# The output product moved to the seam between two stages, and the last expert's lower product carried into the next heads' stage

## What is computed

```python
    h = layernorm(x, ln_g, ln_b)
    q, k, v = heads(h @ Wq), heads(h @ Wk), heads(h @ Wv)
    q = l2norm(q) * q_scale
    k = l2norm(k) * k_scale
    logits = jnp.einsum('bhid,bhjd->bhij', q, k) * QK_SCALE
    attn = jax.nn.softmax(jnp.where(causal, logits, NEG_INF), axis=-1)
    out = jnp.einsum('bhij,bhjd->bhid', attn, v)
    out = out.transpose(0, 2, 1, 3).reshape(B, S, H * DH) @ Wo
    h = layernorm(out, ln_g, ln_b)
    gate = jax.nn.softmax(h @ gate_w + gate_b, axis=-1)
    hid = jax.nn.gelu(jnp.einsum('bsd,edf->bsef', h, w1) + b1)
    exp_out = jnp.einsum('bsef,efd->bsed', hid, w2) + b2
    moe = jnp.einsum('bse,bsed->bsd', gate, exp_out)
    return layernorm(moe, ln_g, ln_b)
```

## Time and profile before

| | before |
|---|---|
| median of 3 runs | 1336.35 us (1336.09 to 1337.26) |
| the profiled execution, its own time | 1336.95 us |
| its span, first to last instruction | 1335.2 us |
| TensorE, products | 1166.4 us busy, 87% |
| TensorE, weight loads | 948.6 us, 71% |
| VectorE | 1017.0 us, 76% |
| ScalarE | 807.9 us, 61% |
| GpSimd | 243.2 us, 18% |
| TensorE's granted clock, mean | 0.931 |

### The profile page before, as it was taken

How to read it: one execution, slowest core, us unless ns; L and a number is a source line. 1 busy time by engine, 2 the same in 40 slices (tenths; PEclk the granted TensorE clock), 3 DMA queues, 4 the chain that set the end, 5 groups by cost and what they waited for, 6 DMA issues and landing times.

```text
span 1335.2 us, 27712 instructions
## 1 busy us (share of the span) xinstructions
PE 1166.4 (87%) x10435; PEld 948.6 (71%) x10435; DVE 1017.0 (76%) x2710; ACT 807.9 (61%) x1868; POOL 243.2 (18%) x283
## 2 busy tenths in 40 slices
PE   3685989897998989899897998989799898989978
PEld 1363768685876868687685877868587786858877
DVE  6669587787878778787877878788887878777652
ACT  5283756658475665747556574755747575575644
POOL 1131211303021030211203021130302113030100
PEclk9595999899999989989899998989999898999889
DMA  6001000000000000000000000000000000000000
GB/s 177 5 1 40 2 1 13 1 9 5 9 5 1 14 1 9 5 9 6 1 13 1 10 5 9 6 1 14 1 9 6 9 5 5 2 9 1 5 5 5
DMA packets 18723, 14.61 MB, mean 11 GB/s; under 512 B 2408, under 2 KB 16160, under 8 KB 18592
## 3 DMA queue, kind: packets, MB, share of 16 engines
q1 hardware_dynamic: 17680, 12.76, 3.3%
q10 hardware_dynamic: 912, 0.09, 0.1%
HBM read 10.75 MB, written 2.10 MB: 10 GB/s over the span
## 4 chain that ended last, share of the span: by engine, by line
PE 69%; ACT 13%; DVE 12%; issue 5%; POOL 0%; SPq 0%; DMA 0%; DVEq 0%; POOLq 0%; ACTq 0%
PE O L499 17%; PE O L415 8%; PE S L398 6%; PE U L431 4%; PE U L483 4%; PE U L484 4%; PE U L485 4%; PE J L344 4%; PE S L362 3%; DVE st L1108 3%; PE S L358 3%; PE J L309 2%; ACT P L676 2%; PE J L311 2%; PE J L310 2%
## 5 line engine op out<-in xcount | busy, mean ns | idle before, releaser
L703 ACT ACTIVATE hid<-U,b1c 128x256 f32<-128x256 f32 x512 | 202.3, 473 | 203.1 <-PE U L485 202.4
L499 PE MATMUL O<-w2s,hid 128*128 128x128 f32 x2048 | 251.5, 276 | 0.0
L499 PEld LDWEIGHTS O<-w2s,hid 128*128 128x128 f32 x2048 | 238.5, 192 | 2.9
L827 POOL TENSOR_SCALAR_AFFINE_SELECT P<-P 128x512 f32<-128x512 f32 x128 | 81.5, 637 | 871.2 <-ACT P L676 871.2
L415 PE MATMUL O<-Vx,P 128*128 128x66 f32 x1536 | 198.1, 279 | 16.5 <-ACT OT L682 16.3
L415 PEld LDWEIGHTS O<-Vx,P 128*128 128x128 f32 x1536 | 181.7, 192 | 32.8 <-issue 24.3
L1108 DVE TENSOR_TENSOR_SCAN st<-aexp,u 128x256 f32<-128x256 f32 x256 | 199.3, 778 | 4.8 <-ACT aexp L688 4.8
L819 POOL TENSOR_TENSOR raw<-raw,nr 128x512 f32<-128x512 f32 x128 | 141.4, 1133 | 141.1 <-DVE nr L981 114.7
L483 PE MATMUL U<-h2h,w1h 128*128 128x256 f16 x512 | 148.7, 290 | 0.2 <-ACT hid L703 0.2
L484 PE MATMUL U<-h2l,w1h 128*128 128x256 f16 x512 | 148.2, 289 | 0.0
L485 PE MATMUL U<-h2h,w1l 128*128 128x256 f16 x512 | 147.5, 288 | 0.0
(11 more groups left out here) (162 smaller groups left out, 2151.2 us busy)
## 6 DMA issues: line engine op xcount, KB each, us to landing
xin<-in_L_attn_x SPq DMA_DIRECT2D x16, 128.0 KB, 2.1
xres<-in_L_attn_x SPq DMA_DIRECT2D x16, 128.0 KB, 2.3
hid<-in_L_ffn_w SPq DMA_DIRECT2D x2, 1024.0 KB, 6.0
out_dram<-fin SPq DMA_DIRECT2D x16, 128.0 KB, 1.8
raw<-in_L_ffn_Wq SPq DMA_DIRECT2D x1, 512.0 KB, 4.4
raw<-in_L_ffn_Wk SPq DMA_DIRECT2D x1, 512.0 KB, 5.6
raw<-in_L_ffn_Wv SPq DMA_DIRECT2D x1, 512.0 KB, 6.6
wos<-in_L_ffn_Wo SPq DMA_DIRECT2D x1, 512.0 KB, 11.0
```

The source lines that it names most:

```text
L499: last = mm(O[e % 2][:, t * P:(t + 1) * P], hid[:, e % 2, m, t * P:(t + 1) * P], w2s[:, e * FC + m, :], start=(m == 0), stop=(m == FC - 1))
L703: fn(hid[:, e % 2, f % FC, :], U[q % 2][:, m * SEQ:(m + 1) * SEQ], ACT.Gelu_apprx_tanh, bias=b1c[:, f:f + 1], scale=1.0 / WS).then_inc(gel ...
```

## The change

The output product of sequence i moves out of the next body's steps 0 and 1 to the seam of its own body: TensorE has it at m = 0, behind the first two `turn_qk`, as one piece, and it writes S2 instead of U0. `output` therefore waits for the last exponentials (they read S2), and the first `scores_for_max` waits for the copy z2. `copy_output` moves to m = 0 on ScalarE, and `o_step` 0 and 1 to m = 9 on VectorE.

The lower product of the last expert, and its weighted sum, move from the end of the experts' stage to step k = 0 of the next body, and `turn_y` goes there as well, now through U1.

With these go the parts of the output norm and the gate: `turn_z2` from k = 6 to 3, `gate_logits` from 7 to 5, `root_o` from 4 to 0, `gate_exps` from 9 to 7, and VectorE's tables O_AT, E_AT and SCAN_AT. `o_step` 12 and 13 move from m = 0 to k = 8. The upper product of expert 0 is written at the end of k = 9 rather than at the start of m = 0, which is the same place. At the seam ScalarE has `copy_ot(7)` before the last two V copies and `high(0)` and `high(1)` before the table load and the gelus; VectorE has `low(0)` and `low(1)` before the norm steps.

The diff, cut to its core:

```diff
@@ tensor @@
                 if p == 0:
                     from_one(pe, ex_done, s * NP)
+                    from_one(pe, wo_copied, s)
...
-            def output(s, t, before):
-                if t == 0:
-                    pe.wait_ge(ot_done, (s + 1) * NP)
-                    if before:
-                        pe.wait_ge(gelu_done, s * NE * FC)
-                for m in range(HD // P):
-                    last = mm(U[0][:, t * P:(t + 1) * P], OT[:, m, t * P:(t + 1) * P],
...
+            def output(s):
+
+                pe.wait_ge(ot_done, (s + 1) * NP)
+                pe.wait_ge(ex_done, (s + 1) * NP)
+                for t in range(T):
+                    for m in range(HD // P):
+                        last = mm(S2[:, 0, t * P:(t + 1) * P], OT[:, m, t * P:(t + 1) * P],
...
             def turn_y(s):
                 pe.wait_ge(y_done, (s + 1) * DS)
-                pe.wait_ge(wo_copied, s + 1)
-                for t in range(T):
-                    last = tr(U[0][:, t * P:(t + 1) * P], y[:, s % 2, t * P:(t + 1) * P], ident[:, :])
+                from_one(pe, gelu_done, s * NE * FC)
+                for t in range(T):
+                    last = tr(U[1][:, t * P:(t + 1) * P], y[:, s % 2, t * P:(t + 1) * P], ident[:, :])
...
-                    if old and k < T:
-                        output(i - 1, k, older)
+                    if older and k == 0:
+                        expert_down(i - 2, NE - 1, i * NP)
+                    if old and k == 0:
+                        turn_y(i - 1)
                     if old and k == 3:
-                        turn_y(i - 1)
-                    if old and k == 6:
                         turn_z2(i - 1)
-                    if old and k == 7:
+                    if old and k == 5:
                         gate_logits(i - 1)
                     if k >= 2:
                         turn_o(i, k - 2)
+                    if old and k == 9:
+                        expert_up(i - 1, 0)
                 for m in range(NE + 2):
-                    if old and m == 0:
-                        expert_up(i - 1, 0)
                     if new and m in TURN_AT:
                         turn_qk(i + 1, TURN_AT[m])
                         turn_qk(i + 1, TURN_AT[m] + 1)
+                    if m == 0:
+                        output(i)
...
-                    if old and 1 <= m <= NE:
+                    if old and 1 <= m < NE:
                         expert_down(i - 1, m - 1, (i + 1) * NP)
@@ scalar @@
             def copy_output(s):
                 act.wait_ge(wo_ready, s + 1)
-                fn(z2[:, :, :].rearrange("p t d -> p (t d)"), U[0][:, 0:SEQ], ACT.Copy).then_inc(wo_copied, 1)
+                from_one(act, o_tr, s)
+                fn(z2[:, :, :].rearrange("p t d -> p (t d)"), S2[:, 0, 0:SEQ], ACT.Copy).then_inc(wo_copied, 1)
...
-                    if old and k == 2:
-                        copy_output(i - 1)
...
-                    if older and k == 0:
+                    if older and k == 1:
                         last_norm(i - 2)
-                    if old and k == 4:
+                    if old and k == 0:
                         root_o(i - 1)
...
-                    if old and k == 9:
+                    if old and k == 7:
                         gate_exps(i - 1)
+                copy_ot(i, NP - 1)
                 if new:
                     copy_v(i + 1, 2)
-                copy_ot(i, NP - 1)
-                if new:
                     copy_v(i + 1, 3)
                     norm_qk(i + 1, 1)
+                    high(i + 1, 0)
+                    high(i + 1, 1)
                 with_gelu_and_tanh()
...
+                    if m == 0:
+                        copy_output(i)
@@ vector @@
-            E_AT = {0: (0, 1), 1: (2, 3, 4), 2: (5, 6), 3: (7,)}
+            E_AT = {1: (0, 1), 2: (2, 3, 4), 3: (5, 6), 4: (7,)}
             G_AT = {0: (0, 1), 4: (2,), 8: (3, 4, 5)}
-            O_AT = {3: (0, 1), 5: (2, 3, 4, 5), 7: (6, 7, 8), 8: (9, 10, 11)}
-            SCAN_AT = {1: 0, 2: 1, 4: 2, 6: 3, 7: 4, 8: 5, 9: 6}
+            O_AT = {1: (2,), 2: (3, 4, 5), 4: (6, 7), 5: (8,), 6: (9, 10, 11), 8: (12, 13)}
+            SCAN_AT = {1: 0, 3: 1, 5: 2, 6: 3, 7: 4, 8: 5, 9: 6}
...
+                    if older and k == 0:
+                        add_expert(i - 2, NE - 1)
...
-                    if old and k == 5:
+                    if old and k == 4:
                         add_y(i - 1)
...
-                    if old and m == 0:
-                        o_step(i - 1, 12)
-                        o_step(i - 1, 13)
...
                         if new and m == 0:
+                            low(i + 1, 0)
+                            low(i + 1, 1)
                             norm_step(i + 1, 1, 1)
...
+                    if m == 9:
+                        o_step(i, 0)
+                        o_step(i, 1)
```

More of the change, by code:

```diff
@@ L423, in turn_o @@
                 last.then_inc(ot_ready, 1)
-            def output(s, t, before):
-                if t == 0:
-                    pe.wait_ge(ot_done, (s + 1) * NP)
-                    if before:
-                        pe.wait_ge(gelu_done, s * NE * FC)
-                for m in range(HD // P):
-                    last = mm(U[0][:, t * P:(t + 1) * P], OT[:, m, t * P:(t + 1) * P],
-                              wos[:, m, :], start=(m == 0), stop=(m == HD // P - 1))
-                if t == T - 1:
-                    last.then_inc(wo_ready, 1)
+            def output(s):
[4 more added lines that the diff above has]
+                        last = mm(S2[:, 0, t * P:(t + 1) * P], OT[:, m, t * P:(t + 1) * P],
+                                  wos[:, m, :], start=(m == 0), stop=(m == HD // P - 1))
+                last.then_inc(wo_ready, 1)
             def turn_y(s):
                 pe.wait_ge(y_done, (s + 1) * DS)
-                pe.wait_ge(wo_copied, s + 1)
+                from_one(pe, gelu_done, s * NE * FC)
                 for t in range(T):
-                    last = tr(U[0][:, t * P:(t + 1) * P], y[:, s % 2, t * P:(t + 1) * P], ident[:, :])
+                    last = tr(U[1][:, t * P:(t + 1) * P], y[:, s % 2, t * P:(t + 1) * P], ident[:, :])
                 last.then_inc(y_tr, 1)
@@ L444, in turn_z2 @@
                 pe.wait_ge(o_vec, s * KO + 10)
-                pe.wait_ge(xy_done, s + 1)
+                from_one(pe, gelu_done, s * NE * FC)
                 for t in range(T):
@@ L451, in gate_logits @@
                 pe.wait_ge(o_vec, s * KO + 11)
+                pe.wait_ge(xy_done, s + 1)
                 for t in range(T):
@@ L583, in tail @@
             def tail():
-                output(LAST, 0, True)
-                output(LAST, 1, True)
+                expert_down(LAST - 1, NE - 1, NSEQ * NP)
                 turn_y(LAST)
@@ L785, in body @@
                         gelus(i - 1, m)
-                    if new and m in TURN_AT:
+                    if m == 0:
+                        copy_output(i)
+                    if new and m > 0 and m in TURN_AT:
                         high(i + 1, TURN_AT[m])
@@ L798, in tail @@
                 last_norm(LAST - 1)
-                copy_output(LAST)
                 root_o(LAST)
@@ L1147, in add_y @@
                 from_one(dve, e_vec, s * KE)
-                V.tensor_tensor(xy[:, :, :].rearrange("p t d -> p (t d)"), U[0][:, 0:SEQ],
+                V.tensor_tensor(xy[:, :, :].rearrange("p t d -> p (t d)"), U[1][:, 0:SEQ],
                                 xb[:, :, :].rearrange("p t d -> p (t d)"), ALU.add).then_inc(xy_done, 1)
@@ L1248, in body @@
                 for m in range(NE + 2):
-                    if old and m == 0:
-                        o_step(i - 1, 12)
-                        o_step(i - 1, 13)
                     if old and m == 2:
                         o_step(i - 1, 15)
-                    if old and m >= 2:
+                    if old and 2 <= m <= NE:
                         add_expert(i - 1, m - 2)
@@ L1287, in body @@
                         step_inputs(i + 1, 1)
+                    if m == 9:
+                        o_step(i, 0)
+                        o_step(i, 1)
             def tail():
+                add_expert(LAST - 1, NE - 1)
                 for n in range(8):
@@ L1292, in tail @@
                 add_y(LAST)
-                for n in range(16):
+                for n in range(2, 16):
                     o_step(LAST, n)
```

## The result

The changed kernel takes **1253.08 us**, the median of four runs (1251.98 to 1255.17), beside 1336.22 for the kernel before: a ratio of 0.938, 95% interval 0.9363 to 0.9397. The prediction was 1266.7, in a range of 1250 to 1300. The profiled execution took 1251.98, with a span of 1250.3, so the span fell by 84.9, where the sum had 69.6.

The account below looks back on a forecast made before the run. TensorE sets the pace almost everywhere, except where it waits in the heads' last steps and at the seam. Gains 63.7 + 6.7 - 0.8 = 69.6 off 1336.95 give 1267.3, as median 1266.7; range 1250 to 1300.

Parts of the forecast that it names:

- VectorE's row up to gateT: Seam, before gated_b2: add_state, scan, add_state beside GpSimd's products take 3.7; with low(2), low(3), gateT is ready at 43.8.
- Steps 0 to 6 and 6 to 9: Heads' stage: scores of step 6 at 19.8 instead of 21.31, then VectorE's shorter row gives turn_o(7) at 33.0 instead of 35.96.
- The seam: Output product fills the 3.86 wait, ending wait and low clock; third turn_qk at 39.35 instead of 42.44.
- What is late next: Before gated_b2: a new wait of about 1.4 for gateT; gated_b2 at 43.9 instead of 47.87, 4.0 gained.
- Experts: From gated_b2 TensorE is dense, 27.93 unchanged; wait of about 1.5 for the maxima, next t = 0 at 73.65.
- Sum: Whole kernel: thirteen steady sequences gain 63.7, sequence 1 gains 6.7, sequence 0 nothing, the last loses 0.8; total 69.6.
- (a): TensorE's clock falls at the new waits, t = 0 and gated_b2, costing 39; 1306 us, chance 0.12.
- (b): ScalarE sets the heads' steps, 0.2 late in seven steps, 1.4 per sequence; 1285 us, chance 0.12.
- (c): Before gated_b2, GpSimd blocks VectorE more than taken, 1.2 per sequence, 17 us; 1284 us, chance 0.08.
- (d): New waits are smaller: VectorE instructions partly clear of GpSimd, maxima earlier; up to 1.2 less per sequence, 1251 us, chance 0.12.
- (e): Move doesn't fill the seam: low(0) not ready when the product ends, about 2 lost; 1300 to 1320 us, chance 0.04.
- (f): Slower than before: lower clock from t = 0 and from gated_b2 in every sequence; 1351 us, chance 0.04.

Follow-up runs that it names:

- experiment 5: Kernel before with only the new seam order: high(0), high(1) ahead of ScalarE's table load, low(0), low(1) ahead of VectorE's norm steps; 1332.7 us (0.9974).
- experiment 2: Changed kernel with the last expert's lower product put back to the end of the experts' stage on TensorE only; 1247.22 us (0.9347).
- experiment 7: Two separate edits of the changed kernel: copy gateT ahead of low(2), low(3), 1242.66 us; three norm steps moved behind scan 8 and its add, 1246.46 us.
- experiment 6: Kernel before with the new ScalarE and VectorE seam order, plus the copy gateT ahead of low(2) and low(3); 1291.92 us (0.967).
- second kernel of experiment 1: Changed kernel with seven eighths of the output product left out, so it computes less; 1251.19 us (0.9375).

## Why the prediction held, step by step

The mechanism held at every place. One term of the sum was mis-sized, VectorE's row up to gateT, and with it two announced figures were missed on the good side: a wait of 1 to 2 before gated_b2 (0.65) and a period of 73.3 to 74.1 (72.71).

| t in one steady sequence | before | predicted | after |
|---|---|---|---|
| scores of step 6 | 21.31 | 19.8 | 19.76 |
| turn_o(7) | 35.96 | 33.0 | 33.01 |
| first turn_qk | 37.54 | 34.6 | 34.59 |
| output product | | 35.6 | 35.47 |
| third turn_qk | 42.44 | 39.35 | 39.04 |
| gated_b2 | 47.87 | 43.9 | 42.86 |
| next t = 0 | 78.58 | 73.65 | 72.71 |

- **Steps 0 to 6 and 6 to 9**: right to a tenth. VectorE waits for the norm's root until 591.78 (t = 22.92; 19.8 + 3.16 was the step), and then works through to On(7) and turn_o(7) at 33.01. Against the kernel before, steps 0 to 6 gave 1.55 and steps 6 to 9, where h2T, h2h and h2l had left VectorE's row, another 1.40.
- **The seam**: right. The third turn_qk came 0.31 before the forecast, because the output product, 3.74 by its record, takes 3.57 from its start to the next one's. The wait for QTl and the low clock are gone, the product lies in their place, and the copy z, begun at 608.17 (t = 39.31), comes ahead of TensorE.
- **What is late next**: this is the step that failed in size. It announced a new wait of 1.4 for gateT, and the wait is 0.65, with gated_b2 1.04 earlier than worked out. The term was three instructions beside GpSimd's products, 3.7. Only two were: the first add_state started at 606.90, ahead of GpSimd's 607.07, and took 0.48; scan and second add took 1.53 and 1.08, as in the earlier trace rows. From start to end that is 3.05 instead of 3.7, and it began 0.26 earlier (t = 38.04 instead of 38.3). 0.9 of the 1.0 is that.
- **Experts**: right. The wait of 1.54 at t = 0 was forecast as 1.5.
- **Sum**, from the starts of the sequences in the two traces: thirteen steady sequences gave 74.8, 5.76 each, where 63.7 stood. The eleven microseconds are, in the main, the mis-sized term, 13 x 0.9. (The forecast took the 78.58 of one sequence for all; the thirteen took 78.48 on the mean, with the low clock in different places, which is 1.3 less to gain.) One sequence of the thirteen, at 277, took 73.72, with a wait of 1.66 before gated_b2. Sequence 1 gained 7.6 (6.7 forecast). Prologue and sequence 0 gained 1.0 (0, bounds -1 and +2). The last sequence with the tail gained 1.5, where a loss of 0.8 stood. In part that is the clock: before, it was low ahead of that sequence's gated_b2 (0.57 from 1256 to 1264), and after it is 1.00 there (1172 to 1181), and gated_b2 comes 1.0 earlier. The rest stays open. The wait before z2's transposes in the tail grew from 3.04 to 6.18, where it was forecast to shrink by 1: the output product no longer stands ahead of it.

**The rivals.** (a), the clock at the new waits, didn't come: 1.00 throughout with waits of 1.54 and 0.65. That it could was no idle thought: experiment 5 has waits of 1.50 and 2.38 at one seam, and the low clock behind them. (b), ScalarE in the heads' steps, cost nothing: TensorE's waits for OT in one sequence are 0.39 and 0.57 after, both where VectorE's row sets the pace, and were 0.34, 0.17 and 0.56 before; in the first steps one is seen only in experiment 2, at 0.34. (c), a whole GpSimd product in front of each VectorE instruction, fell: 0.85 and 0.60 were added, beside products of 1.01 (4.04 for four in experiment 7, where no scan or add lies beside them). (d), smaller waits, is what happened; its number was 1251, its chance 0.12, and one of its two reasons, instructions partly clear of GpSimd, was the right one; the other, the maxima done earlier, was not (1.54). (e) and (f) didn't come.

**The port that VectorE and GpSimd share.** The Trainium skill, "SBUF — State Buffer", section "SBUF: two separate sides", names the cases in which VectorE and GpSimd exclude each other, one of which is a VectorE instruction with two inputs in SBUF. The rows agree in kind: scan and add, with both inputs in SBUF, were stretched; QTl<-J,wcol,QTh, whose large input J is in PSUM, took 0.47 at 609.87 while GpSimd was still in its products, as it does without them (650.62 in the earlier trace rows, behind their end). That the loser fully blocks for the instruction would have put up to 1.01 in front of each; the rows have 0.85 and 0.60, and GpSimd itself lost 0.75 over the four products (4.79 against 4.04).

## What to carry to other kernels

A wait of the busiest engine that comes every round is room for work of that engine: a product that was priced at 3.1 per round in one place cost nothing in the other, and the cut of the same product in both kernels showed it. When such a wait is filled, price the row of the next engine instruction by instruction, and check the start of each against the start of its rival for the port, since one instruction that slipped ahead was 0.6 of the 1.0 by which gated_b2 was mis-timed. And don't judge an edit by the whole time while the clock of TensorE moves: the new order at the seam was worth 2.7 us of the kernel before alone and 43 us with one more line moved, and only half of the difference, 1.4 of 2.9 us per sequence, was the wait that this line shortened.

## What the runs showed of the hardware

- **The low clock can hide a gain.** In experiment 5 a gain of 2.05 per sequence, seen at gated_b2, ended as 0.5, because the stretch of low clock moved from a place where it cost 1.0 to dense products where it cost 1.5.
- **When it falls stays open.** TensorE had waited 0.54, 1.50 and 2.38 at the seam before it fell in experiment 5; with 0.54, 1.49 and 1.00, in experiment 6, it stayed at 1.00 in ten sequences in a row. Before the change it fell after waits of 0.55 and 3.86. But the waits of experiment 5 were followed by full clock in the sequence from 995.25, and there it had fallen a little after 1026, with no wait above 0.57 since that sequence began. In the second kernel of experiment 1 it fell behind waits of 1.05 and 1.28 in some sequences and not in others. So the length of one wait doesn't decide it.
- **A table load costs ScalarE 1.28 us here, and the next instruction starts at once** (605.43, then the gelu at 606.73; before, 643.41 and 644.71). The Trainium skill, "ScalarE: Activation LUTs", section "What ACT_TABLE_LOAD costs", puts a drain of about 1380 ns beside the load; neither trace shows one behind it.
- **VectorE beside GpSimd**: a scan of 256 columns 1.53 instead of 0.68, an add 1.08 instead of 0.48, both with all inputs in SBUF; low halves, with one input in PSUM, unchanged.
